# A second layer whose engine programs are written out for all 32 iterations, in place of a loop over pairs of iterations

## What is computed

```python
def step(h, inp):
    xt, dtt, Bt, Ct = inp
    dA = jnp.exp(dtt[..., None] * A)
    h = dA * h + dtt[..., None] * Bt[:, None, :] * xt[..., None]
    y = jnp.einsum('bdn,bn->bd', h, Ct)
    return (h, y)
...
y = _selective_scan(xs, dt, A, Bm, Cm, D)
y = y * jax.nn.silu(z)
return jnp.einsum('bld,od->blo', y, out_proj_w)
...
return spatial + spectral + ym
```

## Time and profile before

| what | before |
|---|---|
| time, median of 3 executions | 6037.74 us (6035.82 to 6040.58) |
| the profiled execution's own time | 6037.74 us |
| its span, first to last instruction | 6035.0 us |
| first layer | to about 3950 us |
| second layer, first product L1184 to the end | 4008.4 to 6035.0 us |
| mean granted TensorE clock | 0.976 |

### The profile page before, as it was taken

The page is one execution under the profiler, slowest core; times in us unless marked ns, Lnnn a source line. Parts: engine busy times, 40 slices in busy tenths (PEclk is TensorE's granted clock), DMA queues, the critical chain, the costliest instruction groups (busy, mean ns, idle before and its releaser), DMA issues. The chain is left out here.

```text
span 6035.0 us, 91036 instructions
## 1 busy us (share of the span) xinstructions
PE 5545.1 (92%) x27184; PEld 2521.5 (42%) x27184; DVE 4842.5 (80%) x7122; ACT 3699.3 (61%) x7290; POOL 4212.8 (70%) x3213
## 2 busy tenths in 40 slices
PE   7999999999999999999999999968878888788787
PEld 3444444444444444444444444423333333333332
DVE  7777777777777777777777777559999999999998
ACT  3665666666666666666666666656666666666665
POOL 2777766676776677676667776647877778778787
PEclk8999999999999999999999999989999999999999
DMA  4011010110110101101100000035444444444444
GB/s 134 21 43 41 23 35 24 46 35 29 41 34 24 41 28 36 43 27 32 33 13 23 18 11 13 21 124 175 157 159 157 165 164 156 159 158 165 163 156 149
DMA packets 292556, 464.85 MB, mean 77 GB/s; under 512 B 72384, under 2 KB 95808, under 8 KB 290624
## 3 DMA queue, kind: packets, MB, share of 16 engines
q1 hardware_dynamic: 292064, 459.37, 23.4%
HBM read 381.41 MB, written 76.28 MB: 76 GB/s over the span
## 5 line engine op out<-in xcount | busy, mean ns | idle before, releaser
L560 POOL TENSOR_TENSOR sums<-exps 128x512 f32<-128x512 f32 x2048 | 2620.5, 1302 | 1310.9 <-ACT exps L493 1306.0
L569 DVE TENSOR_REDUCE mpart<-ps 128x1 f32<-128x512 f32 x4096 | 2541.9, 683 | 820.2 <-PE ps L369 820.1
L493 ACT ACTIVATE exps<-ps 128x512 f32<-128x512 f32 x4096 | 2127.6, 602 | 1404.4 <-PE ps L376 1404.0
L369 PE MATMUL ps<-k_st,q_ring 96*128 96x512 f32 x4096 | 1754.4, 429 | 17.5 <-DVE v_stage L606 7.9
L1235 POOL TENSOR_TENSOR hc<-hh,c_rep 128x512 f32<-128x512 f32 x1024 | 1363.3, 1339 | 438.2 <-DVE hh L1198 436.1
L376 PE MATMUL ps<-q_ring,k_st 98*128 98x512 f32 x4096 | 1620.7, 397 | 4.0 <-ACT exps L493 3.6
L1198 DVE TENSOR_TENSOR_SCAN hh<-d_a,carry,ps 128x512 f32<-128x512 f32 x1024 | 1298.1, 1270 | 1.1
L369 PEld LDWEIGHTS ps<-k_st,q_ring 96*128 96x128 f32 x4096 | 774.8, 189 | 1064.3 <-DVE mpart L569 547.6
L387 PE MATMUL ps<-exps,v_ring 128*32 128x512 f32 x8192 | 1090.8, 605 | 0.0
L376 PEld LDWEIGHTS ps<-q_ring,k_st 98*128 98x128 f32 x4096 | 778.0, 190 | 148.1 <-ACT exps L493 17.3
L1024 PE MATMUL ps<-s_u,sel_g 128*128 128x512 f32 x1024 | 586.5, 574 | 247.5 <-DVE hh L1198 246.7
(11 more groups left out here) (106 smaller groups left out, 3045.5 us busy)
## 6 DMA issues: line engine op xcount, KB each, us to landing
d_a<-dt_dram SPq DMA_DIRECT2D x1040, 256.0 KB
qk_split<-hilo SPq DMA_DIRECT2D x128, 256.0 KB, 2.3
q_ring<-qk_split SPq DMA_DIRECT2D x384, 64.0 KB, 2.0
k_st<-qk_split SPq DMA_DIRECT2D x45, 512.0 KB, 7.0
dt_dram<-dt SPq DMA_DIRECT2D x33, 512.0 KB, 2.8
za<-z_ext SPq DMA_DIRECT2D x33, 320.0 KB, 3.9
zp<-z_ext SPq DMA_DIRECT2D x32, 320.0 KB, 6.7
xc<-in_x SPq DMA_DIRECT2D x32, 256.0 KB, 2.9
```

Of the source, the lines that this page charges most:

```text
L369: nc.tensor.matmul(d_bank(("max", m, t)), q_ring[0:PARTS, m % 4, 128 * i:128 * i + 128], k_st[0:PARTS, g % 2, chunk(kc)], start=True, stop ...
L493: nc.scalar.activation(exps[:, u % 4, CH * half:CH * half + CH], a_bank(("exp", n, t)), ACT.Exp, scale=SCALE).then_inc(a_done, 1)
L560: pool.tensor_tensor(sums[:, u % 8, :], exps[:, u % 4, 0:CH], exps[:, u % 4, CH:2 * CH], ALU.add).then_inc(summed, 1)
L569: nc.vector.tensor_reduce(mpart[:, m % 2, t % 4, t // 4:t // 4 + 1], d_bank(("max", m, t)), AX.X, ALU.max).then_inc(d_done, 1)
```

## The change

`steps` loses the hardware loop and writes out all 32 iterations, with the parity of the iteration as the buffer number. Since `it` is now always a number, the tests for "is it a number" go, and so does the parameter for the engine. No computation, no buffer, no wait and no order within an iteration is changed, and SP's program stays as it was. The core of the diff (the other places drop `isinstance(it, int)` or the first argument of `steps` in the same way):

```diff
         def ge(e, s, value):
 
-            if not isinstance(value, int) or value > 0:
+            if value > 0:
                 e.wait_ge(s, value)
...
-        def steps(e, prepare, emit, tail):
+        def steps(prepare, emit, tail):
 
             for g in range(G):
                 prepare(0, 0, g)
-            for it in range(2):
-                emit(it, it)
-            with e.Fori(1, NIT // 2) as k:
-                for r in range(2):
-                    emit(k * 2 + r, r)
+            for it in range(NIT):
+                emit(it, it % 2)
             tail()
...
-                        if not (isinstance(it, int) and it == 0):
+                        if it:
                             if g == 5:
                                 add_skip(it - 1, 1 - p, 1)
...
-                steps(dve, prepare, emit, tail)
+                steps(prepare, emit, tail)
```

More of the change, by code:

```diff
@@ L1031, in emit @@
                         prepare(it + 1, 1 - p, g)
-                        if g in (0, 4) and not (isinstance(it, int) and it == 0):
+                        if g in (0, 4) and it:
                             sum_states(it - 1, 6 + g // 4)
-                        if g in (12, 13) and not (isinstance(it, int) and it == 0):
+                        if g in (12, 13) and it:
                             out_proj(it - 1, g - 12)
@@ L1048, in tail @@
                         out_proj(NIT - 1, i)
-                steps(pe, prepare, emit, tail)
+                steps(prepare, emit, tail)
             @block.scalar
@@ L1129, in emit @@
                             last_state(it, p, g - KEEP)
-                        elif not (isinstance(it, int) and it == 0):
+                        elif it:
                             last_state(it - 1, 1 - p, G + g - KEEP)
                         prepare(it + 1, 1 - p, g)
-                        if g == 16 and not (isinstance(it, int) and it == 0):
+                        if g == 16 and it:
                             output(it - 1, 1 - p)
@@ L1137, in output @@
                     act.wait_ge(o_ready, it + 1)
-                    if not (isinstance(it, int) and it < 2):
+                    if it >= 2:
                         act.wait_ge((o_even, o_odd)[p], (it - p) * 8)
@@ L1148, in _ @@
                 nc.scalar.preload_act_table_set(LN_EXP)
-                steps(act, prepare, emit, tail)
+                steps(prepare, emit, tail)
             @block.vector
@@ L1238, in emit @@
                             gate(it, p, 0)
-                        if g == 6 and not (isinstance(it, int) and it == 0):
+                        if g == 6 and it:
                             gate(it - 1, 1 - p, 1)
@@ L1243, in tail @@
                     gate(NIT - 1, 1, 1)
-                steps(pool, prepare, emit, tail)
+                steps(prepare, emit, tail)
         clear(nc, names)
```

## The result

| what | before | after |
|---|---|---|
| median | 6037.17 us (6035.82 to 6040.58, 4 executions) | 5986.84 us (5985.08 to 5988.07, 4 executions) |
| the profiled execution's own time | 6037.74 us | 5988.07 us |
| its span | 6035.0 us | 5986.3 us |
| mean granted TensorE clock | 0.976 | 0.982 |
| instructions executed | 91036 | 84041 |

The ratio is 0.9916, with a 95% interval of 0.9898 to 0.9933: 50.3 us faster. The forecast was 5985.0.

What follows compares the result with a forecast made beforehand. DVE was taken to bound the second layer. From 6037.74 us, -52.2 (jump back), +1.3 (low-clock waits) and -1.8 (rest) gave 5985.0 us, range 5978 to 6000.

Steps and rivals of the forecast that it cites:

- What bounds the kernel: Second layer: DVE sets the pace, busy 60.87 of 61 us an iteration; others' idle time counts only if DVE waits.
- Point 1, the jump back: DVE's first product after each of 14 jumps back waits 3.73 us, all on the path; removing it gives -52.2 us.
- Point 2, waits for PE at the low clock: DVE's product waiting for PE's L1024, 0.43 us each: 8 of 30 iterations instead of five, +1.3 us.
- The rival of "most iterations": PE's low clock delays DVE in most of 30 iterations, up to 12.9 us instead of 2.1: 5994.5 us; chance 0.15.
- Point 3, the rest: DVE's register instructions in the loop and the start again after a gap both go: -1.8 us.
- The sum: Second-layer terms -52.2 + 1.3 - 1.8 = -52.7 us, taken from the profiled execution's 6037.74: 5985.0 us.
- Costed at nothing: ACT's 4.87 us gap, POOL's wait, other engines' register instructions and PE's about 38 more fetches: taken as 0 us.
- the rival of starvation: PE starves on instructions at L1024, holding DVE 2.0 us at each of 38 more fetches: 6061 us; chance 0.03.
- The rival of stalls at borders: Written-out DVE code stops 3.73 us at each fetched block's border, say 8 times: about 6015 us; chance 0.06.
- The figure of 108 ns for a branch: Skill page's compare-and-branch cost; by it alone 14 jumps cost 1.5 us and the change is worth next to nothing.
- The loop body, 293 instructions: Length of DVE's loop body, used to argue against border stalls: fetched anew each lap without gaps within a lap.

Runs made afterwards that it cites:

- loop_pad_48: Kernel before, loop kept, with 48 one-column writes added in DVE's program ahead of the second layer: 6036.11 us, ratio to before 1.0002.
- loop_aligned: Kernel before, all four loops kept, DVE's body cut to 366 instructions by fewer waits and shifted by 73 writes to touch three blocks: 5988.03 us, ratio 0.9924.
- loop_all_but_dve: Changed kernel with the loop put back on ACT, PE and POOL, DVE written out: 5986.11 us, ratio to before 0.9919.
- The short loops: Changed kernel with six 4-lap loops of writes added on DVE before the second layer, in two kernels run once each: 6234.05 and 6286.88 us.

## Why the prediction was right, and what was off

*What bounds the kernel.* Right. DVE sets the pace: looping the three other engines cost nothing, looping DVE cost the whole gain.

*Point 1, the jump back, -52.2 us.* Right in size and place. The waits of "issue" are gone from DVE, and come back with its loop (51.4 us in 14).

*Point 2, waits for PE at the low clock, +1.3 us.* The mechanism was right and the size was not. I took 8 waits of 0.43 us, chosen between two counts. There were 16 of 0.55 us: 8.8 us instead of 3.4. The count was low by both of the rows that I had, 5 in 30 and 5 of the 15 iterations that no jump precedes. It depends on DVE's gap more than on PE's loop: the waits lists have 4 with only DVE looped and 17 with all but DVE looped. It is not the gap alone, since loop_pad_48, with gaps, and loop_aligned, without, both have 10. Why the low clock falls where it does is not shown. The price was low mainly because 61.67 was set against an iteration of 61.24, one that follows a gap, and not against 61.15; the waits were also longer, 0.43 us each where they had been 0.34. The rival of "most iterations" (5994.5) was half right: half the iterations, and 5986.8 lies between it and the forecast.

*Point 3, the rest, -1.8 us.* From iteration 1 to 31 the kernel after takes 1842.5 us. Fifteen waits lie in that stretch, 15 x 0.55 = 8.2, which leaves 1834.3 against the 1834.5 assumed. Right.

*The sum.* Between these two starts 1890.6 - 1842.5 = 48.1 us were gained, where 52.7 were forecast; the 4.6 short is point 2 (4.8) less 0.2 by point 3. That the time still came within 1.9 us of the forecast is in part luck, from small terms that it didn't have. Iteration 1 began 0.96 us earlier (4067.81), the tail was 0.34 longer, and the profiled executions' times lie 2.76 and 1.78 us above their spans: 48.07 + 0.96 - 0.34 + 0.98 = 49.67, which is 6037.74 - 5988.07. And the median after is 1.2 us below that execution.

*Costed at nothing.* ACT's stop: right. In loop_all_but_dve it stays, with no gap of DVE beside it, and DVE's groups don't wait for ACT. PE's 39 fetches (38 were forecast) cost nothing, and with them the rival of starvation falls. DVE has no "issue" wait at block borders either, so the 0.33 us of a border seen in dense writes does not show at the kernel's pace. The rival of stalls at borders supposed 8 of them. There were more, about one an iteration: in the same 1700 us queue q14 has 105 packets in loop_all_but_dve and 76 in loop_aligned, so DVE's written-out program took 29 of them.

*The figure of 108 ns for a branch* from the Trainium skill, Advanced Engine Details and Errata, section Control Flow Timing. The short loops restart 0.3 to 0.5 us after the last write, wait included, so nothing here speaks against the figure for the branch alone; it does not give what a jump costs when the body must be fetched again. The Trainium skill, Runtime: NRT & Kernel Launch, section Instruction fetch mechanics, says that a taken branch outside the window forces a fetch. That it is a fetch, which I had left open, the packet counts now show.

*A wrong number.* "The loop body, 293 instructions": it is 426. The 2206 after the change, 69 for an iteration, comes from the same listed order; the trace has 136 records of DVE for a written-out iteration. The argument drawn from the 293, that the body is fetched anew in each lap, held, and with 426 the packets fit: 5.9 a lap are DVE's five blocks and one more, and the other 5.6 of the 11.6 a lap are there in loop_aligned too.

## What to carry to other kernels

On DVE here a hardware loop paid a refetch at every jump back when its body touched four or more blocks of 128 instructions, and nothing when it touched three. So count the executed records between two branches of the bounding engine, waits and register work included, and compare with that. Either write the loop out, or cut and place the body so that it fits: both gave the same time here. Look at the bounding engine first: a stop of 4.8 us on ACT, which ran ahead of DVE, cost nothing.

## What was unexpected

The place of a body decides: 366 instructions in three blocks cost nothing a jump, in four 3.7 us a jump, and in four with a border 6 instructions after the start 3.6 + 2.5 = 6.1 us a jump. A loop can so lose 38 us (6038 to 6076) by 50 instructions more or less ahead of it. Why the body shifted by 120, which starts at 97 and touches five blocks like the kernel before, has gaps of 4.2 to 4.5 us in place of 3.7 is open. Whether ACT and POOL hold as many blocks as DVE was not tried.
